# Four expert stages: the down product turned, in split float32r terms, one output per 512 tokens

## The reference

```
L0:  out += mask * ((silu(x gw_e.T) * (x uw_e.T)) dw_e.T) * mean_w    8 experts, hidden 512
L1:  (silu(x wg.T) * (x wu.T)) wd.T                                  1 "expert", hidden 384
L2:  x + sum_topk gate * ((relu(x wg_e) * (x wp_e)) wo_e)            8 experts, hidden 256
L3:  out += w_e * (relu(x w1_e + b1_e) w2_e + b2_e)                  8 experts, hidden 256
```

## Time and profile before

| | |
|---|---|
| median of three runs | 2433.44 us |
| profiled execution: time, span | 2440.75 us, 2438.9 us |
| TensorE, VectorE, ScalarE, GpSimd busy | 85%, 68%, 43%, 22% of the span |
| mean granted TensorE clock | 0.889 |
| stage 1, first to last `hidden` matmul | 255.2 to 546.5 us |
| stage 2 | 954.1 to 979.6 us, end of its last addition 9.7 us after its last item's start |
| stage 3 | 1552.7 to 1697.1 us, its last item from 1696.31 |
| stage 4 | 2326.6 to 2426.2 us |

### The profile page before, as it was taken

One profiled execution on the slowest core, in us unless ns is written; L12 is line 12 of the kernel. 1 busy time (PEld: TensorE's weight loads), 2 busy tenths in 40 slices (PEclk: granted clock), 3 DMA queues, 4 the chain that ended last, 5 costly groups with the idle time before them and its releaser, 6 DMA issues. The chain is left out here.

```text
span 2438.9 us, 36556 instructions
## 1 busy us (share of the span) xinstructions
PE 2066.0 (85%) x12192; PEld 1383.0 (57%) x12216; DVE 1662.4 (68%) x4273; ACT 1045.7 (43%) x2326; POOL 533.2 (22%) x905
## 2 busy tenths in 40 slices
PE   6698899998999897767774997598699979999888
PEld 3455788884555455433332554587334348777777
DVE  5666677786675576779997565456679856666655
ACT  2354222222564453455551344322367734444333
POOL 0342110102110530068883321010211010000010
PEclk8698899997897799889996798799689979999989
DMA  8321000004120420000003220000511110000000
GB/s 338 99 60 23 1 1 1 1 1 130 44 53 18 121 60 2 1 1 0 1 1 105 73 48 8 1 1 1 174 36 46 33 44 1 1 1 1 1 1 18
DMA packets 60073, 94.61 MB, mean 39 GB/s; under 512 B 11313, under 2 KB 33137, under 8 KB 58737
## 3 DMA queue, kind: packets, MB, share of 16 engines
q1 hardware_dynamic: 29312, 55.29, 6.7%
q0 software_dynamic: 29952, 36.45, 6.2%
q10 hardware_dynamic: 624, 0.54, 0.1%
HBM read 65.50 MB, written 31.29 MB: 40 GB/s over the span
## 5 line engine op out<-in xcount | busy, mean ns | idle before, releaser
L1008 DVE TENSOR_REDUCE m<-banks 128x1 f32<-128x512 f32 (+3 forms) x512 | 272.6, 584 | 94.6 <-PE banks L1172 54.4
L2687 PEld LDWEIGHTS banks<-w_ffn,eh 128*128 128x128 f32 x2144 | 279.2, 191 | 23.5 <-DVE eh L2628 1.9
L2687 PE MATMUL banks<-w_ffn,eh 128*128 128x128 f32 x2144 | 281.2, 274 | 1.5 <-DVE eh L2628 1.5
L1140 ACT ACTIVATE p<-banks 128x512 f32<-128x512 f32 (+3 forms) x512 | 234.0, 522 | 101.4 <-PE banks L1218 58.7
L1443 DVE TENSOR_REDUCE m<-banks 128x2 f32<-128x308 f32 x384 | 165.7, 475 | 137.1 <-PE banks L1743 70.3
L2675 PE MATMUL banks<-x_hi,w_hi 128*128 128x512 f32 x472 | 211.2, 447 | 17.4 <-PEq L332 17.4
L1170 PE MATMUL banks<-K,Qf 32*128 32x512 f32 (+2 forms) x512 | 182.5, 515 | 14.6 <-PEq L332 9.9
L2657 ACT ACTIVATE et<-banks 128x512 f32<-128x512 f32 x140 | 83.6, 597 | 246.8 <-PE banks L2677 203.2
L2677 PE MATMUL banks<-x_hi,w_lo 128*128 128x512 f32 x472 | 188.7, 400 | 0.0
L2676 PE MATMUL banks<-x_lo,w_hi 128*128 128x512 f32 x472 | 187.6, 397 | 0.0
L1216 PE MATMUL banks<-Q,K 32*128 32x512 f32 (+2 forms) x512 | 153.5, 499 | 14.9 <-ACT p L1140 13.0
(11 more groups left out here) (423 smaller groups left out, 4332.7 us busy)
## 6 DMA issues: line engine op xcount, KB each, us to landing
Qf<-stack_q_plain POOLq DMA_DIRECT2D x48, 256.0 KB, 3.0
Qf<-stack_q_masked POOLq DMA_DIRECT2D x32, 256.0 KB, 3.0
K<-stack_k_self POOLq DMA_DIRECT2D x32, 256.0 KB, 3.1
w_ffn<-ffn_dram SPq DMA_DIRECT2D x1, 6144.0 KB, 35.2
stack_q_plain<-q_hi SPq DMA_DIRECT2D x24, 256.0 KB, 3.1
stack_q_masked<-q_hi SPq DMA_DIRECT2D x16, 256.0 KB, 3.0
stack_k_self<-k_hi SPq DMA_DIRECT2D x16, 256.0 KB, 3.8
K<-stack_k_ctx POOLq DMA_DIRECT2D x48, 80.0 KB, 2.7
```

Of the source, the lines that this page charges most:

```text
L1008: ins = dve.reduce_max(k.m[:, t, h:h + 1], bank[:, 0:(t + 1) * P if k.kind == "page" else S], AX)
L1140: nc.scalar.activation(k.p[:, x % PBUFS, q0:S], score_banks[x % 3][:, q0:S], ACT.Exp).then_inc(sem("exp_done"), 1)
L2687: last = pe.matmul(bank[:, t * P:(t + 1) * P], k.h[:, n % RING, t * P:(t + 1) * P], w(down.format(e))[:, i * P:(i + 1) * P], start=(i == 0 ...
```

## The change

The down product is turned round: `output(n)` takes the down weight as the stationary operand and h over 512 tokens as the moving one, in three float32r matmuls (L2776 to L2778 of the new file). That needs h and the down weights in high and low parts. ScalarE casts h to its high part (`high`, L2708), and GpSimd (stages 1 to 3) or VectorE (stage 4) subtracts for the low part (both under the name h_lo). GpSimd also cuts the down weights (`cut_down`, L2577, L2579). The output now has features on partitions: ScalarE copies it out (`take_output`, in stage 4 with the bias b2, L2717), TensorE transposes it back in four float32 transposes per pair (`turn_output`, L2783), and then VectorE adds it. `output` runs three items behind `hidden` and `turn_output` five. Stage 3 joins the last three experts, stage 4 the last two; stage 2 prepares one batch of the next normalization instead of two; the result is stored in four transfers as batches are done. Some semaphores are renamed. In full, but for `hidden` on VectorE (same operations, now waiting for `h_parts`) and renamings:

```diff
-FFN3["b2"] = (E8 * P, lambda i: np.broadcast_to(row(i["L3_ffn_b2"]), (P, E8 * P)))
+FFN3["b2"] = (E8, lambda i: i["L3_ffn_b2"].T)
...
+HRING, LAG, TAKE = 4, 3, 4
...
+    def __init__(self, net, sb, act_kind, tiles, rings):
         self.kinds = 1 if act_kind == "bias" else 2
-        self.wring = 2 * tiles
+        self.tiles, self.rings = tiles, rings
+        self.wring = rings * tiles
         self.x_hi, self.x_lo = sb("x_hi", [P, B * S], F32R), sb("x_lo", [P, B * S], F32R)
         self.w_hi, self.w_lo = sb("w_hi", [P, self.wring, self.kinds * P], F32R), sb("w_lo", [P, self.wring, self.kinds * P], F32R)
-        self.t = sb("et", [P, 2, S])
-        self.a = sb("ea", [P, 2, S])
-        self.h = sb("eh", [P, RING, S])
-        if act_kind == "bias":
-            self.y = sb("ey", [P, 2, S])
+        self.d_hi, self.d_lo = sb("d_hi", [P, self.wring, P], F32R), sb("d_lo", [P, self.wring, P], F32R)
+        self.h_hi, self.h_lo = sb("h_hi", [P, HRING, S], F32R), sb("h_lo", [P, HRING, S], F32R)
+        self.h, self.y = sb("eh", [P, RING, S]), sb("ey", [P, S])
+        turned = net.xnT_all[:].rearrange("p (i q) -> p i q", q=S)
+        self.t, self.a = turned[:, 0:2], turned[:, 2:4]
...
+def cut_down(net, pool, k, name, e, i):
+    n, done = (e * k.tiles + i) % k.wring, e * k.tiles + i + 1
+    src = net.w(name.format(e))[:, i * P:(i + 1) * P]
+    if e >= k.rings:
+        pool.wait_ge(net.sem("h_used"), ((e - k.rings + 1) * B - 1) * k.tiles + i + 1)
+    pool.tensor_copy(k.d_hi[:, n], src).then_inc(net.sem("d_hi_ready"), 1)
+    pool.wait_ge(net.sem("d_hi_ready"), done)
+    pool.tensor_tensor(k.d_lo[:, n], src, k.d_hi[:, n].bitcast(F32), ALU.subtract).then_inc(net.sem("d_ready"), 1)
+    pool.wait_ge(net.sem("d_ready"), done)
...
-    apart = experts - min(experts, 2) if ahead else experts
+    joined = ahead > 0 or store is not None
+    apart = max(0, experts - max(2, k.rings - 1)) if joined else experts
     pairs = [(e, b) for e in range(apart) for b in range(B)]
     pairs += [(e, b) for b in range(B) for e in range(apart, experts)]
     work = [(m, i) for m in range(len(pairs)) for i in range(tiles)]
     pieces = DOUBLE_PIECES if norm_kind == "double" else PIECES
-    stretch = (experts - apart) * tiles
-    begin = apart * B * tiles + stretch + 2
+    stretch = max((experts - apart) * tiles, pieces)
+    begin = (apart * B + experts - apart) * tiles + LAG + 3
+    pool_lows = act_kind != "bias"
+    hidden_banks = 2 if tiles == 2 and k.kinds == 2 else 3
+    y_banks = ps[6:8] if tiles > 2 else ps[4:8]
+    ny = len(y_banks)
+    lead = min(2, k.rings - 1)
+    def cuts(e, at):
+        if e >= apart:
+            return [(e + 1, at)] if lead == 1 and e == apart and at < tiles and e + 1 < experts else []
+        new = [(f, j) for f in range(1 if e == 0 else e + lead, e + lead + 1 + (e == apart - 1 and k.rings > 3)) if f < experts for j in range(tiles)]
+        late = 0 if e == 0 else 3
+        step = max(1, (B * tiles - late) // max(1, len(new)))
+        c, rest = divmod(at - late, step)
+        return [new[c]] if rest == 0 and 0 <= c < len(new) else []
...
-            for e in range(1, experts):
-                cut_weights(net, pool, k, first, tiles, e, (e - 1) * tiles)
+            for i in range(tiles):
+                cut_down(net, pool, k, down, 0, i)
+            for n, (m, i) in enumerate(work):
+                e, b = pairs[m]
+                if pool_lows:
+                    pool.wait_ge(sem("h_high"), n + 1)
+                    nc.gpsimd.tensor_tensor(k.h_lo[:, n % HRING], k.h[:, n % RING], k.h_hi[:, n % HRING].bitcast(F32), ALU.subtract).then_inc(sem("h_parts"), 1)
+                for new, j in cuts(e, b * tiles + i):
+                    cut_weight(net, pool, k, first, new, j, (new - 1) * tiles)
+                    cut_down(net, pool, k, down, new, j)
+            pool.wait_ge(sem("h_parts"), len(work))
...
-                dve.wait_ge(sem("h_used"), tiles * (m + 1))
+                dve.wait_ge(sem("turned"), m + 1)
                 if (e - 1, b) in pairs:
                     dve.wait_ge(sem("x_added"), pairs.index((e - 1, b)) + 1)
-                y = ps[6 + m % 2][:].rearrange("p (t d) -> p t d", t=QT)
-                if act_kind == "bias":
-                    own = k.y[:, m % 2].rearrange("p (t d) -> p t d", t=QT)
-                    ch.link(dve.tensor_tensor(own, y, over(w("b2")[:, e * P:(e + 1) * P], 1, QT), ALU.add))
-                    y = own
+                y = y_banks[m % ny][:].rearrange("p (t d) -> p t d", t=QT)
...
+            def low(n):
+                dve.wait_ge(sem("h_high"), n + 1)
+                dve.tensor_tensor(k.h_lo[:, n % HRING], k.h[:, n % RING], k.h_hi[:, n % HRING].bitcast(F32), ALU.subtract).then_inc(sem("h_parts"), 1)
             for n, (m, i) in enumerate(work):
                 if act_kind != "bias":
...
+                    hidden(n)
+                else:
+                    low(n)
+                if n >= LAG + 3 and work[n - LAG - 3][1] == tiles - 1:
+                    add_expert(work[n - LAG - 3][0])
+                b, piece = divmod(n - begin, stretch)
                 if 0 <= b < ahead and piece < pieces:
                     norm_piece(b, piece)
+            left = range((len(work) - LAG - 3) // tiles, len(pairs))
...
+            def high(n):
+                act.wait_ge(sem("h_ready"), n + 1)
+                if n >= HRING:
+                    act.wait_ge(sem("h_used"), n - HRING + 1)
+                nc.scalar.copy(k.h_hi[:, n % HRING], k.h[:, n % RING]).then_inc(sem("h_high"), 1)
+            def take_output(m):
+                act.wait_ge(sem("h_used"), tiles * (m + 1))
+                if m >= 1:
+                    act.wait_ge(sem("turned"), m)
+                e = pairs[m][0]
+                if act_kind == "bias":
+                    taken = nc.scalar.activation(k.y[:], y_banks[m % ny][:], ACT.Identity, bias=w("b2")[:, e:e + 1])
+                else:
+                    taken = nc.scalar.copy(k.y[:], y_banks[m % ny][:])
+                taken.then_inc(sem("y_taken"), 1)
...
+                if n >= 1:
+                    high(n - 1)
+                if n >= TAKE and work[n - TAKE][1] == tiles - 1:
+                    take_output(work[n - TAKE][0])
...
+                at = (e * tiles + i) % k.wring
+                pe.wait_ge(sem("d_ready"), e * tiles + i + 1)
+                pe.wait_ge(sem("h_parts"), n + 1)
+                if i == 0 and m >= ny:
+                    pe.wait_ge(sem("x_added"), m - ny + 1)
+                y_bank = y_banks[m % ny]
+                h_hi, h_lo = k.h_hi[:, n % HRING], k.h_lo[:, n % HRING]
+                pe.matmul(y_bank[:], k.d_hi[:, at], h_hi, start=i == 0, stop=False)
+                pe.matmul(y_bank[:], k.d_lo[:, at], h_hi, start=False, stop=False)
+                pe.matmul(y_bank[:], k.d_hi[:, at], h_lo, start=False, stop=i == tiles - 1).then_inc(sem("h_used"), 1)
+            def turn_output(m):
+                pe.wait_ge(sem("y_taken"), m + 1)
                 for t in range(QT):
-                    last = pe.matmul(bank[:, t * P:(t + 1) * P], k.h[:, n % RING, t * P:(t + 1) * P], w(down.format(e))[:, i * P:(i + 1) * P],
-                                     start=(i == 0 and t == 0), stop=(i == tiles - 1), skip_group_check=True)
-                last.then_inc(sem("h_used"), 1)
-            for n in range(len(work) + 2):
+                    last = pe.transpose(y_banks[m % ny][:, t * P:(t + 1) * P], k.y[:, t * P:(t + 1) * P], w("ident"))
+                last.then_inc(sem("turned"), 1)
+            for n in range(len(work) + LAG + 2):
                 if n < len(work):
                     hidden(n)
-                if n >= 2:
-                    output(n - 2)
+                if n >= LAG + 2 and work[n - LAG - 2][1] == tiles - 1:
+                    turn_output(work[n - LAG - 2][0])
+                if n >= LAG and n - LAG < len(work):
+                    output(n - LAG)
+        @block.sync
+        def _(sp):
+            if store is None:
+                return
+            out, stored = store
+            for b in range(B):
+                sp.wait_ge(sem("x_added"), pairs.index((experts - 1, b)) + 1)
+                sp.dma_start(out[:, b * QT:(b + 1) * QT, :], x_of(net, b)).then_inc(stored, 16)
+            sp.wait_ge(stored, 16 * B)
...
-        experts(None, None, "silu", ("L1_w", "L1_d"), 1, 3, norm_kind="one", ahead=2)
+        experts(None, None, "silu", ("L1_w", "L1_d"), 1, 3, rings=1, norm_kind="one", ahead=1)
...
-        experts("f2_router", route_sinkhorn, "relu", ("w{}", "d{}"), E8, 2, keep_x=True, norm_kind="double", ahead=2)
+        experts("f2_router", route_sinkhorn, "relu", ("w{}", "d{}"), E8, 2, rings=4, keep_x=True, norm_kind="double", ahead=2)
...
-        experts("f3_router", route_tokens, "bias", ("w{}", "o{}"), E8, 2)
+        experts("f3_router", route_tokens, "bias", ("w{}", "o{}"), E8, 2, store=(ov, stored))
...
```

(76 more changed lines are left out.)

65 lines of the change are left out of this document (24 added, 41 removed).

## The result

The changed kernel took 2460.3 us (median of four runs, 2451.79 to 2467.25), the kernel before 2432.68 (four runs): a ratio of 1.0098, interval 1.0055 to 1.0142. Run again beside experiments 5 to 8 it gave 1.0121 (1.0081 to 1.0160). So it is slower by 1%, 27.6 and 28.8 us; 2465 and "slower" were predicted, in a range of 2438 to 2488. The profiled execution took 2456.45 us.

The account below looks back on a forecast made before the run. TensorE was taken to set the pace in all stages. Stages 1 to 4 at -3.6, +2.6, +7.1 and +25.5 sum to +31.6 us: 2472 profiled, 2465 on the median's footing, 8-in-10 range 2438 to 2488.

Parts of the forecast that it names:

- Bound: All expert stages: TensorE sets the pace, busy for the whole of each stretch in the rows read.
- Product and transposes: TensorE: product -0.21 us per item, four transposes 0.44 per pair; stage 1 2.28 to 2.17 (-14 us), stage 3 stays 2.28.
- Stage 4, the loop: Stage 4: gate, relu, cast, copy, transposes make two items take 3.98 us instead of 3.17, 30 times, +24 us.
- Rival A: Stage 4: ScalarE's copy is in time, so TensorE's 1.60 us per item holds; 2441 us, 17%.
- Last expert's cuts: GpSimd cutting the last expert in four successive stage 1 items, 3.45 us each against 2.17: +1.7 us after slack.
- Joined stretches: Normalization pieces on VectorE wait for GpSimd at the shared port: stage 1 +2.0 lost gain, +2.5 waits; stage 3 +2.0.
- Start: Starts of stages 1 and 3: cuts of the next experts stand between the first low parts, +1.0 and +1.4 us.
- Ends: Longer chain from a stage's last item to its end: stage 1 +3.2, stage 3 +0.8, stage 4 +1.5 us.
- The block behind stage 2: Block after stage 2 has one batch more to normalize, with statistics for four tiles: +2.3 us.
- Rivals B: All stages: the covers hold everywhere, only TensorE's sum counts, not slower; 2423 us, 6%.
- C: Stage 1 and joined stretches: GpSimd becomes the bound, +17 us, port waits +18, about 2490 us; 12%.
- D: Transposes go one after the other, four costing 1.08 us instead of 0.44, +64 over 100 pairs; 2529 us, 2%.

Follow-up runs that it names:

- experiments 5 to 8: Runs on another chip: two edits of a mix with the new product in stage 1 alone (2427.91, 2433.15 us), changed kernel again (2464.76), kernel before again (2431.22).
- experiment 1: Changed kernel with ScalarE's copy of the output queued ahead of the newest item's relu or tanh, in all stages: 2437.36 us, ratio 1.0018.
- second trace: Second profile of the changed kernel, unedited and run on another chip: 2464.76 us.
- experiment 3: Changed kernel, GpSimd subtracting only 4 of 512 columns for the low part in the joined stretches of stages 1 and 3: 2452.88 us, one run.
- first pair: First profiles of the kernel before and the changed kernel, nothing else edited: spans 2438.9 and 2454.6 us.
- second pair: Profiles of the kernel before and the changed kernel, both run again unedited on another chip: spans 2429.4 and 2463.7 us.
- experiment 5: Kernel before with new product in stage 1 only, copy ahead, stage 4's last experts joined, store per batch, last expert's down cuts four items later: 2427.91 us, ratio 0.9971.

## Why the prediction was right, point by point

- **Bound.** TensorE sets the pace where rows showed it full: right in the middle of stages 1 and 3.
- **Product and transposes.** Four items of stage 1 take 2.50, 2.07, 2.04 and 2.04 us, 2.16 on average, where 2.17 was forecast. An item with transposes costs 0.47 more (0.44 forecast). Two items of stage 3 take 2.49 and 2.06, 2.28 each, as forecast.
- **Stage 4, the loop.** Forecast +24.0, measured +21.1 (120.7 against 99.6): the period is 3.92, not 3.98, and the loop closes 29 times, not 30. Rival A (the copy in time) fell with 29 waits for L2717; experiment 1 made A's condition true and got A's time, 2437 for 2441.
- **Last expert's cuts.** Forecast +1.7, measured 3.1, over three items. The step that was too small is the slack taken off: GpSimd's cycle was right (3.42 for 3.45), but the slack that the low parts have was set at 3.4 us and was about 2. Cuts in stage 3: +1.7 for +2.1.
- **Joined stretches.** Forecast +4.5 in stage 1 (2.0 of lost gain, 2.5 of waits), measured +2.9. Two operations were held for over 1 us, and TensorE stood behind each of them; the gain was not lost on the other items. What was not in the working is the way of the delay: through the cast and then the copy in ScalarE's queue, the loop of stage 4 in another place.
  The Trainium skill, "SBUF — State Buffer", SBUF: two separate sides, has the rule that the prediction gives, that whichever starts first holds the shared pair for the whole instruction: the trace agrees, 1.15 us for 0.16 with the subtraction on GpSimd, 0.16 without it, and the operations with an input in PSUM kept 0.69.
  The prediction counted only operations with two inputs on chip. Some with one were held as well: in stage 2 L401, an operation of 128x4 that otherwise takes 0.17 us, ran from 972.06 for 1.26 us, beside a subtraction from 972.00 to 973.29. So its ten were too few, though none of these made TensorE wait in stage 1.
- **Start.** +1.0 and +1.4 forecast for stages 1 and 3. In stage 1 one item took 2.38 instead of 2.04, so 0.3 (in the second trace 3.28, behind an item that took 1.46 instead of 2.56); in stage 3 about 1.
- **Ends.** Stage 1 +4.0 for +3.2: the item's start to the last addition is 10.4 us where 9.7 was forecast. Stage 3 +1.9 for +0.8: the last subtractions still meet the normalization pieces (L677, 128x4, takes 1.15 us at 1695.87), and experiment 3 took 1.1 us of it away. Stage 4 +0.8 for +1.5; the last addition ended 8.81 us after the last item's start, forecast 8.9. The miss is in the sum: 8.9, 3.0 and 1.7 make 13.6 and not 13.8 (measured 13.5), and the end before is 12.7 in the trace, where its parts were added to 12.3.
- **The block behind stage 2.** +2.8 for +2.3. Stage 2 itself -0.3 for +0.3.
- **Sum.** Stages, their ends and that block: -10.0 + 4.0 - 0.3 + 2.8 + 3.7 + 1.9 + 21.1 + 0.8 = +24.0 in the first pair, against +31.6. The remaining 8.3 us down to +15.7 are in the start and in the layers between. In the second pair the same sum is about +26, and the start and the layers add 8 to it (34.3 us). Rivals B, C and D fell: stage 4 waits, GpSimd is busy 138.5 of 170 us in the middle of stage 1 and never waited for there, and four transposes take 0.60 us. Rival C's price was added up wrongly, too: 17 and 18 us on top of 2465 are 2500, not 2490.

That the forecast came within 5 us of the median owes something to chance: terms on the high side by 7.6 us stood against a start and layers that differ by as much from trace to trace and of whose clock no term spoke. The largest term, and the mechanism that decides the sign, held.

## What to carry to other kernels

Where several engines each run a queue in a fixed order, follow one ring from a product through the others and back, and compare it with the work that covers it; an operation on old data that is queued behind one on the newest data lengthens the ring by both. Put the old data first. Here that took 20 us out of stage 4. A gain of 0.1 us per item (14 us here) is taken back by stalls at seams, so each of them is worth spreading, as experiment 5 did.
